# Reordering the attention steps of a pipelined transformer kernel: scores and the preceding step's value product first, turned probabilities later, normalised rows turned before the key product

## The reference

```
def _layer(x, wqkv, qs, ksc, wo, lg, lb, w1, b1, w2, b2):
    h = shift_token(x)
    q, k, v = split(h @ wqkv)                   # 8 heads of 64
    q = l2norm(q) * qs ; k = l2norm(k) * ksc
    q, k = rotary_xpos(q, k)
    o = local_attention(q, k, v)                # windows of 128 rows, each sees itself and the one before
    x = x + o @ wo
    h = layernorm(shift_token(x)) * lg + lb
    a, g = split(h @ w1 + b1)
    return x + (a * gelu(g)) @ w2 + b2
```

## Time and profile before

| what | value |
|---|---|
| time, median of 3 runs | 3566.89 us (3561.45 to 3569.26) |
| the profiled execution: its time, its span | 3563.92 us, 3562.1 us |
| last two layers, first and last matmul | about 2101.7 us to 3558.1 us of the span |
| PE busy, whole span | 3319.4 us (93%) |
| DVE, ACT, POOL busy, whole span | 60%, 49%, 16% |
| granted clock, whole span | 0.972 |

### The profile page before, as it was taken

One profiled execution on the slowest core, in us unless ns is written; L12 is line 12 of the kernel. 1 busy time (PEld: TensorE's weight loads), 2 busy tenths in 40 slices (PEclk: granted clock), 3 DMA queues, 4 the chain that ended last, 5 costly groups with the idle time before them and its releaser, 6 DMA issues. The chain is left out here.

```text
span 3562.1 us, 51625 instructions
## 1 busy us (share of the span) xinstructions
PE 3319.4 (93%) x18018; PEld 1923.0 (54%) x18018; DVE 2125.5 (60%) x6268; ACT 1731.8 (49%) x3299; POOL 562.1 (16%) x698
## 2 busy tenths in 40 slices
PE   8999999999997788999999658999999999999998
PEld 3455555555555434544444435566666666666665
DVE  3243343343346557677765547777777777777773
ACT  2233333333333366566555325655656666555562
POOL 0000000000002333434431211111111111111110
PEclk9999999999999799999999879999999999999999
DMA  4110111101100200000000030000000000000000
GB/s 180 54 63 30 40 37 44 63 30 39 54 13 13 82 6 11 7 16 14 11 13 13 9 138 19 18 22 22 22 25 22 22 21 28 29 28 27 22 29 20
DMA packets 77898, 120.69 MB, mean 34 GB/s; under 512 B 10222, under 2 KB 66227, under 8 KB 72520
## 3 DMA queue, kind: packets, MB, share of 16 engines
q1 hardware_dynamic: 77640, 117.38, 9.7%
HBM read 96.35 MB, written 16.83 MB: 32 GB/s over the span
## 5 line engine op out<-in xcount | busy, mean ns | idle before, releaser
L2669 PE MATMUL wps<-w_wqkv,w_hT 128*128 128x512 f32 x768 | 378.3, 617 | 3.1 <-DMA w_wo<-in_wwo 3.1
L2268 POOL TENSOR_TENSOR w_rn<-w_n,w_mhalf 128x16 f32<-128x16 f32 x64 | 189.2, 2956 | 1053.1 <-DVE w_n L2459 1053.1
L2707 PE MATMUL wps<-w_xnT,w_w 128*128 128x512 f32 (+1 forms) x704 | 319.6, 597 | 24.5 <-DVE w_xnT L2522 20.5
L1219 POOL TENSOR_TENSOR b_routs<-b_rins,b_expo 128x4 f32<-128x4 f32 x88 | 90.6, 1032 | 1496.1 <-DVE b_rins L1439 1496.1
L2296 ACT ACTIVATE w_pr<-w_sm,w_nmx,w_rn 128x256 f32<-128x256 f32 (+1 forms) x512 | 286.6, 562 | 9.1 <-DVE w_nmx L2440 8.4
L656 PE MATMUL ps<-xT,b_late 128*128 128x512 f32 x512 | 245.8, 603 | 0.0
L672 PE MATMUL ps<-hid,b_late 128*128 128x512 f32 x512 | 240.8, 593 | 0.0
L2707 PEld LDWEIGHTS wps<-w_xnT,w_w 128*128 128x128 f32 (+1 forms) x704 | 132.1, 190 | 188.5 <-issue 164.8
L1284 ACT ACTIVATE bb_pr<-ps 128x1024 f32<-128x1024 f32 x128 | 130.4, 1018 | 180.0 <-PE ps L1814 179.6
L2669 PEld LDWEIGHTS wps<-w_wqkv,w_hT 128*128 128x128 f32 x768 | 137.9, 193 | 131.9 <-issue 126.9
L298 ACT ACTIVATE hid<-ps,rb 128x512 f32<-128x512 f32 x128 | 87.9, 687 | 223.2 <-PE ps L656 223.0
(11 more groups left out here) (333 smaller groups left out, 6804.1 us busy)
## 6 DMA issues: line engine op xcount, KB each, us to landing
b_late<-in_ew SPq DMA_DIRECT2D x32, 1024.0 KB, 6.8
w_xa<-xs SPq DMA_DIRECT2D x16, 512.0 KB, 3.9
w_xin<-xs SPq DMA_DIRECT2D x64, 128.0 KB, 4.2
xT<-in_xT SPq DMA_DIRECT2D x8, 512.0 KB, 3.8
xres<-in_x SPq DMA_DIRECT2D x32, 128.0 KB, 2.2
x<-x1t SPq DMA_DIRECT2D x32, 128.0 KB, 1.7
b_mod<-ada SPq DMA_DIRECT2D x16, 256.0 KB, 3.2
xs<-bb_wb SPq DMA_DIRECT2D x8, 512.0 KB, 2.8
```

Source lines behind the costliest of these rows:

```text
L2268: g.tensor_tensor(rn[:, i % 2, t], n2[:, n % 2, 1], mhalf[:], ALU.pow).then_inc(nr_ok, 1)
L2669: ins = te.matmul(to, hT[:, i % 2, k, t * P:(t + 1) * P], wqkv[:, i // B, k, s * 512:(s + 1) * 512], start=(k == 0), stop=(k == KD - 1))
L2707: ins = te.matmul(to[0:n], w1[:, i // B, k, lo:lo + n], xnT[:, k], start=(k == 0), stop=(k == KD - 1))
```

## The change

Three things are done, all in `window_layers`. First, the order of a step on TensorE was T, S, q or tq, O, then k or projection and v; it becomes S, O of the preceding step, q or tq, T, (xn), then k or projection and v. ScalarE and VectorE follow: their copies of the turned probabilities stand later in a step, ScalarE's copy of a chunk's heads moves to the next, even step, and their copies of the turned normalised rows stand right behind the turned probabilities. Second, xn is turned before the k product and no longer behind it. Third, since O comes one step later, the turned probabilities have two buffers, the values a ring of five chunks where there were four, and to make room the scratch tile of the rotation (`t2`) shares the tile of the squares (`sq`), for which the squares wait for the rotation before (`rope_ok`).

```diff
--- before.py
+++ after.py
@@ -2035,9 +2035,10 @@
         sq = sb("sq", [P, 2 * NH, DH])
         n2 = sb("n2", [P, 2, 2, 2 * NH])
         rn = sb("rn", [P, 2, NT, 2 * NH])
-        t2 = sb("t2", [P, 2, NH, DH])
+        t2 = sq[:].rearrange("p (s h) v -> p s h v", s=2)
         qk = sb("qk", [P, 2, 2, NH, DH])
-        vt = sb("vt", [P, NT, NC * P])
+        VR = NT + 1
+        vt = sb("vt", [P, VR, NC * P])
         qT = sb("qT", [P, NC, L])
         kT = sb("kT", [P, NC, L])
         sm = sb("sm", [P, 4, 2 * P])
@@ -2046,7 +2047,7 @@
         pr = sb("pr", [P, 4, 2 * P])
         rs = sb("rs", [P, 2, 4])
         ri = sb("ri", [P, 2, 4])
-        pT = sb("pT", [P, 2, 2, 2, P])
+        pT = sb("pT", [P, 2, 2, 2, 2, P])
         oT = sb("oT", [P, 2, NC, P])
         xm = sb("xm", [P, 2, NT, D])
         hs = sb("hs", [P, 2, NT, P])
@@ -2142,17 +2143,18 @@
 
             if make_qk(G):
                 yield ("q",) + make_qk(G)
-                yield ("k",) + make_qk(G)
             if turn_qk(G):
                 yield ("tq",) + turn_qk(G)
                 yield ("tk",) + turn_qk(G)
+            if turn_rows(G):
+                yield ("xn", turn_rows(G)[0], 0)
+                yield ("xn", turn_rows(G)[0], 1)
+            if make_qk(G):
+                yield ("k",) + make_qk(G)
             if project(G):
                 yield ("wo",) + project(G)
             if make_v(G):
                 yield ("v",) + make_v(G)
-            if turn_rows(G):
-                yield ("xn", turn_rows(G)[0], 0)
-                yield ("xn", turn_rows(G)[0], 1)
             if gates(G):
                 i, f = gates(G)
                 yield ("g", i, 2 * f)
@@ -2278,9 +2280,9 @@
                 t = G % U // 2
                 k0 = 1 if t == 0 else 0
                 act.wait_ge(pT_mm, G + 1)
-                if G:
-                    act.wait_ge(pv_mm, G)
-                a.activation(pT[:, 0, :, k0:], ps[:, 2].rearrange("p (c k q) -> p c k q", c=2, k=2)[:, :, k0:], ACT.Copy).then_inc(pT_a, 1)
+                if G >= 2:
+                    act.wait_ge(pv_mm, G - 1)
+                a.activation(pT[:, G % 2, 0, :, k0:], ps[:, 2].rearrange("p (c k q) -> p c k q", c=2, k=2)[:, :, k0:], ACT.Copy).then_inc(pT_a, 1)
 
             def exponentials(G):
                 i, u = divmod(G, U)
@@ -2310,13 +2312,15 @@
                 emptied(act, "k", i, t)
                 if n:
                     act.wait_ge(n2_ok, n)
+                    act.wait_ge(rope_ok, n)
                 a.activation(sq[:], qkr[:, n % 2].rearrange("p s h v -> p (s h) v"), ACT.Square).then_inc(sq_ok, 1)
 
             def values(i, t):
                 filled(act, "v", i, t)
-                if i:
-                    act.wait_ge(pv_mm, (i - 1) * U + min(2 * t + 4, U))
-                a.activation(vt[:, t], bank("v", i, t), ACT.Copy).then_inc(free[place["v", i, t][0]], 1)
+                n = i * NT + t
+                if n >= VR:
+                    act.wait_ge(pv_mm, 2 * (n - VR + 1) + 2)
+                a.activation(vt[:, n % VR], bank("v", i, t), ACT.Copy).then_inc(free[place["v", i, t][0]], 1)
 
             def queries(i, t):
                 filled(act, "tq", i, t)
@@ -2365,24 +2369,24 @@
                 a.activation(hT[:, i % 2, 0], bank("x", i, 0), ACT.Copy).then_inc(free[place["x", i, 0][0]], 1)
 
             for G in STEPS:
-                if attends(G):
-                    turned_probabilities(G)
                 if make_qk(G):
                     raw_rows("q", 0, *make_qk(G))
                 if turn_qk(G):
                     queries(*turn_qk(G))
+                if attends(G - 1) and G % 2 == 0:
+                    heads_out((G - 1) // U, (G - 1) % U // 2)
+                if attends(G):
+                    turned_probabilities(G)
+                if turn_rows(G):
+                    normal_rows(turn_rows(G)[0])
                 if make_v(G):
                     squares(*make_v(G))
                 if attends(G + 1):
                     exponentials(G + 1)
                 if make_qk(G):
                     raw_rows("k", 1, *make_qk(G))
-                if attends(G) and G % 2:
-                    heads_out(G // U, G % U // 2)
                 if make_v(G):
                     values(*make_v(G))
-                if turn_rows(G):
-                    normal_rows(turn_rows(G)[0])
                 if gates(G):
                     i, f = gates(G)
                     gelu(i, 2 * f)
@@ -2419,9 +2423,9 @@
                 t = G % U // 2
                 k0 = 1 if t == 0 else 0
                 dve.wait_ge(pT_mm, G + 1)
-                if G:
-                    dve.wait_ge(pv_mm, G)
-                v.tensor_copy(pT[:, 1, :, k0:], ps[:, 3].rearrange("p (c k q) -> p c k q", c=2, k=2)[:, :, k0:]).then_inc(pT_v, 1)
+                if G >= 2:
+                    dve.wait_ge(pv_mm, G - 1)
+                v.tensor_copy(pT[:, G % 2, 1, :, k0:], ps[:, 3].rearrange("p (c k q) -> p c k q", c=2, k=2)[:, :, k0:]).then_inc(pT_v, 1)
 
             def masked_scores(G):
                 i, u = divmod(G, U)
@@ -2476,7 +2480,7 @@
                     ins = v.tensor_tensor(t2[:, :, :, s * HF:(s + 1) * HF], r[:, :, :, (1 - s) * HF:(2 - s) * HF],
                                           rots[:, i // B, 1, t, :, s * HF:(s + 1) * HF].unsqueeze(2).broadcast_to([P, 2, NH, HF]), ALU.mult)
                 ch.link(ins)
-                v.tensor_tensor(qk[:, n % 2], qk[:, n % 2], t2[:], ALU.add).then_inc(rope_ok, 1)
+                v.tensor_tensor(qk[:, n % 2], qk[:, n % 2], t2, ALU.add).then_inc(rope_ok, 1)
 
             def keys(i, t):
                 filled(dve, "tk", i, t)
@@ -2647,8 +2651,8 @@
                     for k in range(k0, 2):
                         for g in range(2):
                             h = 2 * c + g
-                            ins = te.matmul(ps[64 * g:64 * g + 64, 4, c * P:(c + 1) * P], vt[:, t - 1 + k, h * DH:(h + 1) * DH],
-                                            pT[:, g, c2, k], start=(k == k0), stop=(k == 1))
+                            ins = te.matmul(ps[64 * g:64 * g + 64, 4, c * P:(c + 1) * P], vt[:, (i * NT + t - 1 + k) % VR, h * DH:(h + 1) * DH],
+                                            pT[:, G % 2, g, c2, k], start=(k == k0), stop=(k == 1))
                 ins.then_inc(pv_mm, 1)
 
             def turn_inputs(i):
@@ -2722,24 +2726,24 @@
             pe.wait_ge(ld_s, 2 * 16)
             pe.wait_ge(pre_ok, PRE)
             for G in STEPS:
-                if attends(G):
-                    turned_probabilities(G)
                 if attends(G + 1):
                     scores(G + 1)
+                if attends(G - 1):
+                    outputs_of_heads(G - 1)
                 if make_qk(G):
                     input_rows("q", 0, *make_qk(G))
                 if turn_qk(G):
                     turn_heads(*turn_qk(G))
                 if attends(G):
-                    outputs_of_heads(G)
+                    turned_probabilities(G)
+                if turn_rows(G):
+                    turn_normal_rows(turn_rows(G)[0])
                 if make_qk(G):
                     input_rows("k", 1, *make_qk(G))
                 if project(G):
                     project_heads(*project(G))
                 if make_v(G):
                     input_rows("v", 2, *make_v(G))
-                if turn_rows(G):
-                    turn_normal_rows(turn_rows(G)[0])
                 if gates(G):
                     i, f = gates(G)
                     hidden("g", 1, i, 2 * f)
```

## The result

| what | before | after |
|---|---|---|
| time, median (range) | 3567.82 us (3561.45 to 3569.26), 4 runs | 3530.72 us (3530.62 to 3533.11), 4 runs |
| ratio | 1 | 0.9901, interval 0.9884 to 0.9918 |
| span of the profiled execution | 3562.1 us | 3528.8 us |
| period of an item, steady part | 87.68 us | 85.39 us |

The kernel became 1.0% faster; the forecast was 3533 us. The steady part first: busy time over nearly the same stretch as the earlier trace rows, columns as there.

A forecast was written before the change was run, and what follows sets the result against it. PE was taken as the bound; -1.6, -1.54 and +1.1 gave -2.0 us an item, -28.6 over 14 items, and -5 at the end. With 3.0 added for the median, 3533 us was forecast, range 3511 to 3556.

The forecast's parts named there:

- The bound: Last two layers, steady part: PE is the bound, busy 1031.66 of 1048 us.
- The shape changes: PE's step order: three changes of tile shape a step instead of four, -1.6 us an item.
- The bound of 0: Limit of the shape saving on PE: no gain if the crossing is paid elsewhere.
- The turned rows: PE's wait for the turned normalised rows is hidden behind the k product, -1.54 us an item.
- The rotation: PE's transposes tq wait for the late rotation: 0.7, 0.35, 0.05 and none in four step pairs, +1.1 us an item.
- The signs of being wrong: T nearer than 3.9 us to S without q's copy in front, L2684 waiting in steps 3, or bank waits at L2663/L2673.
- The edges and the sum: First two items 0, last item but one -5 us, 14 items -28.6: -33.6 us in all.
- about what it is now: 0: First two items: the loop T, exponentials, rotation, tq, T takes 17.4 us a pair, no change, bounds -5 and +4.
- Full gain: Rival: the rotation is never late because ScalarE's copies overlap more; 3518 us, chance 0.18.
- free crossings: Rival: PE's shape changes are hidden or paid elsewhere, an item gains 1.54 us; 3552 us, chance 0.13.
- the slower one: Rival: the rotation is late in all pairs, VectorE or ScalarE adding 1.2 us a pair; 3592 us, chance 0.08.
- the likeliest case: The forecast itself for the whole kernel, with its own range 3524 to 3544 us, chance 0.55.

The follow-up runs named there:

- rotation first: Changed kernel with the second half of the rotation ahead of the probabilities on VectorE: 3507.79 us, ratio 0.9839.
- the split experiment: Changed kernel with the rotation's second half ahead of the probabilities, plus even steps' value product moved from behind S to behind q: 3519.09 us, ratio 0.9873.
- order alone: Changed kernel with the normalised rows turned behind the key and v products again, their copies behind exponentials and probabilities: 3592.4 us, ratio 1.0068.
- the same swap on the kernel before: Kernel before the change, with the second half of the rotation ahead of the probabilities on VectorE: 3628.45 us, ratio 1.0177.

## Why the prediction was right

**The bound.** PE was and is the bound; in the steady part nothing but PE's waits and its changes of shape moved.

**The shape changes, -1.6 us an item.** Right. With every wait gone the period is 84.51 ("rotation first"), and 87.68 - 1.6 - 1.54 is 84.54. The two parts of the -1.6, 0.09 on leaving and 0.10 on entering, were right for products; in front of transposes entering costs 0.05. The bound of 0, that the crossing is paid elsewhere, is out.

**The turned rows, -1.54.** The wait went as walked. As a price it was read too simply: taken alone the move gives 1.4 in the old order, and left out it costs 2.9 plus clock in the new one. The sum was unaffected, since both parts were changed together.

**The rotation, +1.1.** Right in place, chain and order of size: walked 0.7, 0.35 and 0.05, measured 0.59, 0.25 and 0.03, so 0.87. The steps with and without a wait came as named, and the walk's remark that two branches meet at 8.07 and 8.16 was confirmed by moving each. Both waits were 0.1 short of the walk. In step 7 all of that is there at the reciprocal, which starts 8.09 us behind S where the walk said 8.18: the copies on ScalarE overlap a little more than walked, and the reciprocal starts 0.1 before the first half of the rotation ends, where the walk put it behind. The signs of being wrong that the forecast named are absent: tq does not wait in step 3, and PE waits for no PSUM bank at L2663 or L2673.

**The edges and the sum.** Here two errors cancelled, and that was luck. The forecast counted 14 items at the steady gain, the first two at nothing, and -5 for the end. Twelve of the 14 items are the twelve periods, and the two others lie in the end.

| part | forecast, us | measured, us |
|---|---|---|
| 14 items | -28.6 (2.04 each) | -32.0 (2.28 each) |
| first two items | 0 | +3.4 |
| end, without its two items | -5 | -4.7 (-9.3 less 2 x 2.28) |
| sum | -33.6 | -33.3 |

The end went as walked. In the last item but one, from the turned rows to the next step is 5.65 us (3442.94 to 3448.59) where it was 10.17 (3469.02 to 3479.19), since the pause fell from 4.06 to 1.01 and the clock held.

The step that failed is "about what it is now: 0". It is wrong by 3.4 us, within its bound of +4. The loop through the rotation was walked at 17.4 us a pair and measured at 18.4 to 20.2 (tq at 2165.06, 2184.03, 2204.19, 2222.79 and 2241.14); in the kernel before, the same distance is 17.0 (tq at 2168.97, 2185.96, 2202.95). The walk itself was right at the upper clock level: without the 2.86 us that the groups behind the pause take too long (12.11 against 9.25), the pair of 20.16 is 17.3. But it took every duration at that level, and the matmuls behind a pause of 3 us don't have it. The forecast also priced the start from the 13.0 us of waits in front of T alone. In the same stretch the kernel before waits in front of tq as well, and in the changed kernel all of PE's waits for other engines stand there, 27.5 us in place of 24.6 (13.0, 10.2 and 1.4 for the turned rows). Before and after, 2106 to 2302:

```profile
PE wps L2680 <- DVE w_qk L2479: 10.2, 7, 5.6
```

```profile
PE wps L2684 <- DVE w_qk L2483: 27.5, 10, 5.7
```

**The rivals.** Full gain is out by 0.87 us an item, free crossings by the split experiment, the slower one because the lateness did not add up from pair to pair: the waits of all items are alike. The time lies 2 us from the forecast, within the likeliest case's own range. These 2 us are mostly the 3.0 that the forecast added for the median of the kernel before over its profiled execution; in the changed kernel the two are equal.

## What to carry to other kernels

When an engine is busy 98% of the time, read its order group by group from start to start: what is left is in waits that one line explains and in the gaps between unlike groups. Before moving a step, ask of each result it produces or delays which other chain runs over the same in-order engine, and walk that chain from one anchor with the durations of the trace; here this gave a new wait of 0.9 us to within 0.2, and the repair (the urgent result first) with it. A swap has no value of its own: the same one gained 23 us in one order and lost 63 in the other, and two moves that gave under 0.1 us an item each gave 0.65 together. Where the bound engine comes to wait for long in one piece (2.73 us and more here), count with a lower clock behind it: that was left out here in the forecast of the first items and in two of the expectations.

## What the runs showed of the hardware that was not expected

A pause of TensorE can be paid twice. Behind a wait of 1.36 us the eight passes of 512 columns took 3.67 us in all 12 steady items of the kernel before. Behind a wait of 2.73 us they took 3.67 us in 6 steady items of "order alone" and 5.20 to 6.75 us in 5, with a granted clock of 1.00 or of 0.96 to 0.98 over the item. Behind 3.10 us, in "the same swap on the kernel before", they took 5.37 us in 8 items and 3.67 in 4. So pauses of one and the same length, in items that do the same work, are paid once or twice; what decides it in an item is not shown here. In the first items, waits of over 3 us in one piece went with a clock of 0.89 over 200 us, and mostly shorter ones with 0.93.

The Trainium skill, TensorE: Matmul & The Clock Gate, section HAM oscillation — how this bites in real kernels, warns of such a falling clock behind stalls, and this trace agrees with it in kind.

A change of tile shape cost 0.09 us on leaving the 128x128 shape and 0.05 to 0.10 us on entering it, and the first weight load behind a change started with its own matmul, where it started 0.43 us ahead within a shape. Scores took 1.06 us in front of the value product and in front of q alike, though the value product, like the scores, runs as pairs on two halves of the array.

The Trainium skill, TensorEngine Tiling (Array Packing), section Key Properties, says that a change of tiling mode drains TensorE. The rows agree in that every change had its price and no load ran ahead of it; a drain as such can't be seen in them.
